# Reading an early tile's rows one edge group later in GpSimd's order, in a graph attention and mixture-of-experts kernel

## The reference, cut to what matters

```python
xn = layernorm(x)                                  # x: 3125 nodes x 256
# graph attention, 53125 edges sorted by dst, 4 heads of 64
h = xn @ W;  logits = leaky_relu(a_src[src] + a_dst[dst], 0.2)
alpha = softmax of logits over the edges of each dst
gnn = relu(segment_sum(alpha * h[src], dst) + bias)
x = x + gnn + linear_attention(xn)                 # per node, after all of its edges
# mixture of 8 experts (256 -> 1024 -> 256), top 2 of a gate, gelu
xn2 = layernorm(x);  w = softmax(top_2(xn2 @ Wg + bg))
x = x + sum over e of w[:, e] * (gelu(xn2 @ W1[e] + b1[e]) @ W2[e] + b2[e])
```

## Time and profile before

| | |
|---|---|
| median of 3 executions | 963.41 us (961.66 to 967.51) |
| the profiled execution, its own time | 961.28 us |
| its span in the trace | 959.4 us |
| TensorE matmuls busy | 807.7 us (84%), 4941 instructions |
| VectorE busy | 532.3 us (55%) |
| ScalarE busy | 429.9 us (45%) |
| GpSimd busy | 564.3 us (59%), 580 instructions |
| mean clock granted to TensorE | 0.93 of full speed |

### The profile page before, as it was taken

One profiled execution on the slowest core, in us unless ns is written; L12 is line 12 of the kernel. 1 busy time (PEld: TensorE's weight loads), 2 busy tenths in 40 slices (PEclk: granted clock), 3 DMA queues, 4 the chain that ended last, 5 costly groups with the idle time before them and its releaser, 6 DMA issues.

```text
span 959.4 us, 17908 instructions
## 1 busy us (share of the span) xinstructions
PE 807.7 (84%) x4941; PEld 701.1 (73%) x4942; DVE 532.3 (55%) x1480; ACT 429.9 (45%) x1132; POOL 564.3 (59%) x580
## 2 busy tenths in 40 slices
PE   8986677667487578988999789799999999999994
PEld 7885455445365466776778668689999999999994
DVE  6789787877775887657566868672111111111111
ACT  4656433433353246647666763553333333333330
POOL 2077777777777767777777776565433433333331
PEclk9998999997866779979799999999999999999998
DMA  8347555454456445657476484793665566566561
GB/s 244 120 134 238 140 139 134 139 155 132 130 151 194 129 116 156 195 174 220 148 249 219 126 262 132 186 361 93 146 197 173 167 200 180 167 191 189 164 169 17
DMA packets 81245, 162.48 MB, mean 169 GB/s; under 512 B 11603, under 2 KB 47593, under 8 KB 81049
## 3 DMA queue, kind: packets, MB, share of 16 engines
q1 hardware_dynamic: 50089, 91.32, 29.2%
q0 software_dynamic: 30528, 69.83, 28.6%
q10 hardware_dynamic: 560, 0.52, 0.2%
HBM read 144.12 MB, written 17.51 MB: 168 GB/s over the span
## 4 chain that ended last, share of the span: by engine, by line
PE 43%; POOL 23%; DVE 14%; issue 12%; DMA 5%; DVEq 2%; POOLq 0%; ACT 0%; ACTq 0%
POOL gathered L1082 21%; PE bank L1813 13%; PE bank L1833 13%; PE bank L1660 4%; DMA gathered<-h_table,src_row 3%; DVE gathered L2115 3%; DVE acc L2084 3%; PE bank L1461 2%; PE bank L1647 2%; PE bank L1728 2%; PE bank L1719 1%; PE bank L1743 1%; DVEq L2078 1%; DMA out<-one_hot 1%; PE bank L1801 1%
## 5 line engine op out<-in xcount | busy, mean ns | idle before, releaser
L1082 POOL DMA_INDIRECT gathered<-h_table,src_row x416 | 400.7, 963 | 128.8 <-issue 125.0
L1660 PE MATMUL bank<-gathered,one_hot 128*128 128x260 f32 x832 | 246.0, 447 | 120.4 <-DVE acc L2084 118.0
L1660 PEld LDWEIGHTS bank<-gathered,one_hot 128*128 128x128 f32 x832 | 173.7, 219 | 167.5 <-DVE acc L2084 137.2
L1422 ACT ACTIVATE one_hot<-bank,one_hot 128x128 f32<-128x128 f32 x296 | 84.6, 369 | 172.5 <-PE bank L1813 172.5
L1142 POOL DMA_INDIRECT out<-one_hot x37 | 58.0, 1569 | 158.0 <-DMA out<-one_hot 98.9
L1813 PEld LDWEIGHTS bank<-one_hot,acc 128*128 128x128 f32 x1184 | 138.0, 192 | 2.6 <-ACT one_hot L1414 0.8
L1813 PE MATMUL bank<-one_hot,acc 128*128 128x128 f32 x1184 | 138.4, 275 | 0.5 <-ACT one_hot L1414 0.5
L1833 PE MATMUL bank<-w_sb,one_hot 128*128 x592 | 133.8, 379 | 0.0
L1277 ACT ACTIVATE bank<-z 128x16 f32<-128x16 f32 x104 | 19.4, 186 | 245.8 <-DVE z L2110 245.6
L2115 DVE TENSOR_TENSOR gathered<-gathered,bank 128x1024 f32<-128x1024 f32 x104 | 127.0, 1221 | 4.2 <-ACT gathered L1291 0.9
L2084 DVE TENSOR_TENSOR acc<-acc,bank 64x260 f32 x208 | 87.8, 422 | 70.4 <-issue 52.5
(11 more groups left out here) (371 smaller groups left out, 1067.0 us busy)
## 6 DMA issues: line engine op xcount, KB each, us to landing
acc<-in_L_ffn_W SPq DMA_DIRECT2D x38, 1024.0 KB, 5.0
w_sb<-in_L_ffn_W SPq DMA_DIRECT2D x17, 1024.0 KB, 13.1
w_sb<-key_table SPq DMA_DIRECT2D x52, 256.0 KB, 3.5
gathered<-h_table,src_row POOLq DMA_INDIRECT x416
xs<-in_L_ffn_W SPq DMA_DIRECT2D x4, 1024.0 KB, 6.1
h_table<-acc SPq DMA_DIRECT2D x25, 130.0 KB, 2.0
out<-xs SPq DMA_DIRECT2D x5, 512.0 KB
xn_table<-w_sb SPq DMA_DIRECT2D x5, 512.0 KB, 4.7
```

The source lines that it names most:

```text
L1082: pool.indirect_dma_start(gathered[:, r, j, :], None, h_table, bass.IndirectOffsetOnAxis(ap=src_row[:, t:t + 1], axis=0)).then_inc(gather_ ...
L1422: op = act.activation(hiddenT[:, k, g * P:(g + 1) * P], hidden_bank[2 * k + half][:, f * P:(f + 1) * P], ACT.Gelu, bias=b1_slot[:, k, g:g ...
L1660: mm = pe.matmul(sum_bank[r % SUMS][:, 0:ROW], one_hot[:, r, j, :], gathered[:, r, j, :], start=(j == 0), stop=(j == G - 1))
```

## The change

The condition under which GpSimd issues a tile's read moves by one group. Before, the read of tile `u` stands behind the four gathers of group `TILE_TURN[u] - 2`; after, it stands behind the four gathers of group `TILE_TURN[u] - 1`. The waits ahead of the read move with it. The number of instructions is the same, and so are the data. No other engine's order changes.

```diff
                             pool.indirect_dma_start(gathered[:, r, j, :], None, h_table,
                                                     bass.IndirectOffsetOnAxis(ap=src_row[:, t:t + 1], axis=0)
                                                     ).then_inc(gather_done[r], 16)
-                        if s + 2 in TILE_TURN:
-                            early_rows_in(c, TILE_TURN.index(s + 2))
+                        if s + 1 in TILE_TURN:
+                            early_rows_in(c, TILE_TURN.index(s + 1))
                 pool.wait_ge(early_ready, passes * 2)
```

## The result

| | before | after |
|---|---|---|
| median of 20 executions each, us | 964.62 (961.32 to 970.37) | 961.08 (955.26 to 970.33) |
| ratio, 95% interval | | 0.9957 (0.9936 to 0.9978) |
| span of the profiled execution, us | 959.4 | 956.9 |

The change makes the kernel 4.1 us (0.43%) faster by the ratio; 3.1 us were forecast. That is less than the 1% which the prediction gave as what a measurement can tell, but the interval (2.1 to 6.2 us) excludes zero. Executions over 1.5% above the fastest of their kernel (the 970.33 is one) are left out of the ratios and means.

What follows compares the result with a forecast made beforehand. GpSimd's gather train and TensorE were both taken as near full, with GpSimd's 3.57 us hole on the path. Terms -3.57 + 0 + 0.5 = -3.1 us took 963.41 to 960.3 us, range 955.5 to 965.5.

Steps and rivals of the forecast that it cites:

- Step 3: Sign in the profile after: TensorE idles, or transposes stand longer behind the spread, at tile 3 and hardly elsewhere.
- term 1: GpSimd's 3.57 us idle before tile 0's read, awaiting list `read_l`, is filled by group 58's gathers: -3.57 us, other bound 0.
- The gathers bind at 68 and 69: VectorE waits for gathers there; before group 68 the wait falls to 1 us or less, before 69 it remains.
- The pipeline behind the last gather shifts as a block: Last gather about 3.6 us earlier, near 588; sorting and expert tiles follow as a block, about 3 us earlier.
- the gain is given back: Rival: TensorE, busy without break about 417-444 and 461-494 us, can't follow, or gathers are slow; 963.4 us, chance 0.18.
- term 2: At 12 turns, gathers of group T - 1 come 1.25 us sooner against the train: 0, at best -0.4 us.
- more is gained: Rival: pipeline and train both profit from sooner groups T - 1, up to 5.5 us more, 957 to 954.3; chance 0.11.
- Theory B: From the experiments: the gain comes from groups T - 1 gathered 1.25 us sooner; eleven other moves alone 2 to 5 us faster.
- term 3: Tile reads issued 5.0 us later make TensorE wait for rows, chiefly 1.4 us at tile 3: +0.5 us, 0 to +5.3.
- the rival's own sum: Rows come late: all moved reads land in 5.9 us, 5.4 us left after absorption, 965.2 us; chance 0.13.
- slow gathers in the hole: Rival: four gathers before tile 0's read, each like the longest (1903 ns), add 3.8 us, giving 963.6; chance 0.03.
- clock: Rival: TensorE's 0.58 clock stretch at 457-468 us, worth 4.6 us, vanishes (955.7) or another comes (964.9); 0.04 each way.

## Why the prediction was right

The gain came from where the prediction put it, and the sum, -3.1 us, lies in the measured 2.1 to 6.2. Step 3 failed, though, by the prediction's own signs: it named waits for rows "at tile 3 and hardly elsewhere", and waits at three tiles or more as a sign of being wrong. There are five in each of the three profiles of the changed kernel, 10.9 to 11.3 us in all where 1.4 were forecast. That the time held all the same is in part luck, as the paragraph on the later reads shows.

**The hole** (term 1, -3.57 us). Right in place and sign: the read of tile 0 alone brings 0.9967 and 0.9958, which is 3.2 and 4.1 us. The size was read from one execution, in which the hole happened to be near the middle of what fourteen show.

The list did not have 2.7 us to spare. The rows show 1.28 us from its end to the start of the read (345.20 from the earlier trace rows and 346.48 in the earlier trace rows), which the prediction left out, so the spare was 347.92 - 346.48 = 1.44 us. In the profile after, the list was 1.53 us later and the gathers 2.00 us sooner, and 1.44 - 1.53 - 2.00 = -2.09 is the hole of 2.08 us that was left. In the other six profiles with tile 0's read moved by one group, nothing was left.

**"The gathers bind at 68 and 69".** The forecast for the wait before group 68 was 1 us or less, with the one before 69 remaining. In the profile after it came out the other way round: the wait at 68 is 3.09 us and there is none at 69. In the other two profiles of the changed kernel it is 1.29 us and none, and 0.85 and 0.43.

```profile
408.39 0.18 DVE L2103 TENSOR_TENSOR z<-gathered,ad_sum 128x16 f32<-128x16 f32 x1 [3.09 <-DMA gathered<-h_table,src_row]
412.48 0.17 DVE L2103 TENSOR_TENSOR z<-gathered,ad_sum 128x16 f32<-128x16 f32 x1
```

The step that failed took the arrival of a gather to be its place in the train plus a constant. Group 68 was gathered 4.7 us sooner than before, and its rows were taken only 1.4 us sooner (408.39 against 409.83): from the start of its last gather to the end of the wait it took 7.3 us instead of 4.0. The weight load issued at 400.39 was under way meanwhile, and in the changed kernel with small loads group 68 was taken 4.4 us after its last gather without a wait. But other groups land late there too (group 97 after 6.65 us), so the load is the likely cause at this place and not the only one in the stage.

**The pipeline behind the last gather shifts as a block.** The last gather came 2.2 us sooner in the profile and not 3.6, the sorting 1.8 us sooner, and the span ended 2.5 us sooner. The time from the start of the sorting to the end stayed: 325.7 us before, and 325.0, 328.1 and 324.7 in the three profiles of the changed kernel, which is what other variants show too. Part of the train's lead was lost on the way: from -3.5 us at group 69 it fell to -3.1 and then -2.2, at the two places where a gather took 1.32 and 1.79 us instead of 0.95. In the other two profiled executions of the changed kernel the last gather starts at 587.02 and 587.15, 4.4 and 4.3 us sooner, as forecast and a little more, and the sorting 3.3 and 5.0 us sooner. So the rival "the gain is given back" falls.

**The reordering** (term 2, 0). Right as far as shown: the rival "more is gained" would have needed Theory B, and the eleven other moves alone, which bring the reordering and the late reads together, gain nothing.

**The later reads** (term 3, +0.5, with 0 and +5.3 as bounds, which the rival's own sum puts at 5.4). The mechanism was right and the size of the wait was not. Tile 3 was named, and it waits 2.82 us; the tiles 2, 5 and 9 were put just above the limit, and tiles 5 and 9 wait. Tile 7, which was given 11.5 us from read to transposes before and so 6.5 after, waits longest, 3.56 us: its landing took 7.71 us, and TensorE stood ready 4.3 us after the read's start, not 6.5. Tile 11, put at 5.2 us, waits 1.36. The mis-sized number is the landing: 2.9 us in the median of the earlier trace rows was carried over to the new places, where it is 5.9. I had written that the moved read of tile 3 falls between two loads rather than on one. It falls 2.0 us behind one. Tile 5's read shows how the place decides: in the kernel before it started at 438.45, 2.6 us ahead of the load issued at 441.03, and after at 440.40, 4.0 us behind the load issued at 436.39; it took 4.7 us. The bound from above, all late reads at 5.9 us, was the better description of the rows. What it cost in time was less than that bound (5.4 us), as the comparison with tile 0 alone shows: 1.3 us at most. TensorE's idle time ahead of the sums fell by 7.8 us at the same time; most of the wait for rows took the place of a wait for VectorE. The term's +0.5 thus came out of two errors that cancelled, a wait eight times too short and an absorption that was counted as 2.30 us at most.

By the fit in the Trainium skill's page "DMA: Bandwidth & Descriptors", section "Anatomy of one DMA — SWDGE (gpsimd) path", such a read takes 2.3 us, an estimate. No read of the changed kernel's first profile landed that fast (2.9 us at least), and beside the weight loads the slowest took over three times as long (7.71 us).

**The rival "slow gathers in the hole"** did not decide: the hole was filled by four gathers of 0.95 us. But slow gathers exist elsewhere, see the last section.

**The rival "clock".** The stretch from 457 to 468 us, at 0.58 before, shows 0.82, 0.97 and 0.85 in the changed kernel. It moves by itself, however: 0.71 and 1.00 in two variants whose time is the same, 0.69 and 0.75 with the eleven others alone. Over 350 to 600 us the clock is 0.92 before and 0.93 to 0.94 after.

## What to carry to other kernels

When an engine that runs ahead has a wait for a late result in its queue, put as much independent work ahead of the wait as the result is late. Measure the lateness by the idle time ahead of the waiting instruction, in more than one execution (here it varied from 1.5 to 7.6 us), and move only the instruction that stands in it. Moving its eleven siblings for uniformity brought waits of 10.9 us that happened to be free here. Before moving a small DMA, look for what large transfers are issued at its new place: its time to land belongs to the place, not to the instruction.

## What the runs showed of the hardware

The reads of 128 KB by GpSimd landed in 2.9 us in the median of the kernel before. In the changed kernel's first profile the five reads that were waited for took 4.7 to 7.7 us, and each of them started 0.3 to 4.0 us after a load of 1 MB had been issued on SyncE's queue. With loads of an eighth, two of the same reads were there after 2.9 us.

Most gathers take 0.95 us, a few up to 2.0. In the kernel before and the three profiles of the kernel after, 30 gathers of the edge stage took over 1.2 us, and all of them started while VectorE ran an operation with two large inputs in SBUF: 27 beside the `tensor_tensor` of lines 2128 and 2433 (128x768 or 128x1024), 3 beside line 2476. One from the kernel before, and one from the kernel after:

```profile
179.37 1.22 DVE L2433 TENSOR_TENSOR xs<-xs,w_sb 128x1024 f32<-128x1024 f32 x1
179.78 1.64 POOL L1082 DMA_INDIRECT gathered<-h_table,src_row  x1 [0.30 <-issue]
```
```profile
527.79 1.23 DVE L2128 TENSOR_TENSOR w_sb<-acc,w_sb 128x1024 f32<-128x1024 f32 x1
528.06 1.79 POOL L1082 DMA_INDIRECT gathered<-h_table,src_row  x1 [0.30 <-issue]
```

In the same four profiles 44 gathers started beside the lines 2128 and 2433, and 27 of them are slow. 376 started beside line 2115, a `tensor_tensor` as long, one input of which lies in a PSUM bank, and none of them took over 0.97 us. 20 started beside line 2139, a `scalar_tensor_tensor` of the same size with both inputs in SBUF, and none took over 1.07. The lines with slow gathers beside them all read one input broadcast, which line 2139 does not. So the slow gathers go with the kind of VectorE's operation and not with its being busy. That the one causes the other was not tested by a run.
